# Two-layer recurrence: TensorE multiplies the middle part of layer 1's state ahead of the projection of x instead of behind it

## What is computed

```
a = x[t] @ Wx + b + h @ Wh                       # layer 0, 4 gates
c = sigmoid(a_f) * c + sigmoid(a_i) * tanh(a_g)
h = sigmoid(a_o) * tanh(c)
x1[t] = x[t] + h
m = concat([x1[t], s]) @ W1 + bias               # layer 1, 2 parts
g = sigmoid(m_g + 1);  s = g * s + (1 - g) * tanh(m_c)
out[t] = x1[t] + s
```

## Time and profile before

| | |
|---|---|
| three executions | 228.25, 232.16, 232.23 us; median 232.16 |
| profiled execution | 228.34 us, of which span 226.2 us |
| granted TensorE clock | 0.998 of full speed |
| TensorE busy | 221.1 us (98%), 4850 products |
| weight loads busy | 206.6 us (91%) |
| VectorE busy | 198.8 us (88%), 1555 instructions |
| ScalarE busy | 134.1 us (59%), 903 instructions |
| DMA | 26 GB/s from HBM over the span |

### The profile page before, as it was taken

The page is one execution under the profiler, slowest core; times in us unless marked ns, Lnnn a source line. Parts: engine busy times, 40 slices in busy tenths (PEclk is TensorE's granted clock), DMA queues, the critical chain, the costliest instruction groups (busy, mean ns, idle before and its releaser), DMA issues.

```text
span 226.2 us, 12499 instructions
## 1 busy us (share of the span) xinstructions
PE 221.1 (98%) x4850; PEld 206.6 (91%) x4850; DVE 198.8 (88%) x1555; ACT 134.1 (59%) x903; POOL 3.7 (2%) x12
## 2 busy tenths in 40 slices
PE   7999999999999999999999999999999999999994
PEld 5899999999999999999999999999999999999883
DVE  4889989899899898998998998989989989899895
ACT  3655666656566666665566566665666666656652
POOL 2400000000000000000000000000000000000000
PEclk9999999999999999999999999999999999999999
DMA  6000001010010001000010001101001000000000
GB/s 186 26 17 26 16 26 49 14 29 26 20 45 26 24 20 49 26 16 26 28 39 26 26 14 29 49 14 28 26 21 46 26 26 16 26 16 16 14 14 14
DMA packets 12006, 6.70 MB, mean 30 GB/s; under 512 B 1447, under 2 KB 11693, under 8 KB 11949
## 3 DMA queue, kind: packets, MB, share of 16 engines
q1 hardware_dynamic: 11376, 5.33, 8.4%
q10 hardware_dynamic: 572, 0.59, 0.7%
HBM read 3.82 MB, written 2.10 MB: 26 GB/s over the span
## 4 chain that ended last, share of the span: by engine, by line
DVE 79%; ACT 11%; issue 4%; PE 3%; DMA 1%; ACTq 0%
DVE cell_bank L574 13%; ACT act_bank L492 11%; DVE hT L581 8%; DVE pair L595 7%; DVE x1T L623 7%; DVE acts L603 7%; DVE scan_add L568 7%; DVE h_high L582 6%; DVE u_rest L609 6%; DVE outT L631 6%; DVE pair L597 6%; DVE h_low L588 6%; DMA xT<-in_x_dram 1%; PE a L291 1%; PE a L283 0%
## 5 line engine op out<-in xcount | busy, mean ns | idle before, releaser
L265 PE MATMUL gate_f<-hT,wh_raw 128*128 128x32 f32 x254 | 47.0, 267 | 0.3 <-DVE hT L581 0.2
L265 PEld LDWEIGHTS gate_f<-hT,wh_raw 128*128 128x128 f32 x254 | 37.8, 188 | 9.8 <-DVE hT L581 8.1
L473 ACT ACTIVATE gate_f<-gate_f 128x32 f32<-128x32 f32 x127 | 23.1, 182 | 34.2 <-PE gate_f L265 34.2
L492 ACT ACTIVATE act_bank<-cell_bank 128x32 f32<-128x32 f32 x128 | 23.3, 182 | 33.3 <-DVE cell_bank L574 33.2
L581 DVE TENSOR_TENSOR hT<-out_gate,act_bank 128x32 f32<-128x32 f32 x128 | 23.9, 187 | 21.0 <-ACT act_bank L492 21.0
L498 ACT ACTIVATE acts<-a 128x64 f32<-128x64 f32 x128 | 28.6, 223 | 17.8 <-PE a L291 4.6
L574 DVE TENSOR_TENSOR_SCAN cell_bank<-act_bank,scan_add 128x64 f32<-128x64 f32 x128 | 38.0, 297 | 0.1
L283 PE MATMUL a<-h_high,w1x_scaled 128*128 128x32 f16 x256 | 35.4, 177 | 0.2
L283 PE MATMUL a<-h_high,w1x_third 128*128 128x32 f16 x256 | 35.4, 177 | 0.0
L283 PE MATMUL a<-h_high,w1x_rest 128*128 128x32 f16 x256 | 35.4, 176 | 0.0
L285 PE MATMUL a<-h_low,w1x_fp 128*128 128x32 f16 x256 | 35.4, 176 | 0.0
(11 more groups left out here) (114 smaller groups left out, 1071.9 us busy)
## 6 DMA issues: line engine op xcount, KB each, us to landing
xT<-in_x_dram SPq DMA_DIRECT2D x45, 64.0 KB, 2.0
out_dram<-outT SPq DMA_DIRECT2D x32, 64.0 KB, 1.6
wx_s<-in_L_cond_Wx_dram SPq DMA_DIRECT2D x1, 256.0 KB, 2.9
wh_raw<-in_L_cond_Wh_dram ACTq DMA_DIRECT2D x1, 256.0 KB, 3.3
w_raw<-in_L_cond_weight_dram ACTq DMA_DIRECT2D x1, 256.0 KB, 3.5
xT<-in_x_dram ACTq DMA_DIRECT2D x1, 64.0 KB, 3.3
bias_rows<-in_biases_dram ACTq DMA_DIRECT2D x1, 3.0 KB
condT<-in_cond_dram SPq DMA_DIRECT2D x1, 16.0 KB, 3.2
```

The lines of the kernel that those rows point to most:

```text
L265: nc.tensor.matmul(gate_step(GATE_F, j), wh_raw[:, GATE_F * P:(GATE_F + 1) * P], hT[:, (j - 1) % RING, :], start=False, stop=True, skip_gr ...
L473: return nc.scalar.activation(out, gate_step(q, j), func)
L492: nc.scalar.activation(tanh_c[:, :], cell[:, :, 1], ACT.Tanh).then_inc(tanh_c_ready, 1)
```

## The change

In steps from 2 on, TensorE issues the four products with `u_rest` right behind the six products of the state's upper part, and so ahead of the projection of x at line 233. The two products with `u_low` stay behind the projection. The wait for `u_rest_ready` moves along with the products. No instruction is added or removed, and the other engines' streams are the same.

```diff
                             layer1_input(l)
                             layer1_high(r, l)
+                            layer1_rest(r, l)
 
                     ends = last and m == 1
...
                     if not (first and j < 2):
-                        layer1_rest(r, l)
                         layer1_low(r, l)
```

## The result

| | before | changed |
|---|---|---|
| median | 230.25 us (6 executions, 228.18 to 232.39) | 234.99 us (6 executions, 232.97 to 237.10) |
| profiled execution | 228.34 us, span 226.2 | 232.97 us, span 230.8 |
| eight steps, `hT` to `hT` | 13.43 us | 13.74 us |

The changed kernel is slower: the ratio is 1.0207, with a 95% interval of 1.0187 to 1.0227; whether it is slower by more than 2% is left open by that. The executions of either kernel fall into two groups about 4 us apart (228.2 to 228.3 and 232.2 to 232.4; 233.0 to 233.1 and 236.9 to 237.1), and all ratios of this document compare the lower groups only.

A forecast was written before the change was run, and what follows sets the result against it. Layer 0's 1.67 us chain was taken to bound seven steps of eight; the change makes layer 1's loop of 1.715 us the pace. Sum: 228.34 + 4.35 + 0.3 = 233.0 us, range 230.3 to 237.0.

The forecast's parts named there:

- What bounds the kernel: Before the change: layer 0's 1.67 us chain sets the pace in seven steps of eight, layer 1's in the eighth (1.71).
- the pair's threshold: Layer 1's pair on VectorE, ahead of `keep`: starting later than about 0.47 us after `hT`, it lengthens the step by the excess.
- The loop's sum: Layer 1's loop, pair to pair through u_rest, projection, u_low and tanh: 0.74 + 0.475 + 0.24 + 0.26 = 1.715 us, every step's pace.
- the late step without a projection: Step of the kernel before (u_rest 217.41 to 217.59) giving 0.05 us to the weight load and 0.125 to the next product.
- The 15 eights: Steps 2 to 124, counted as 120 at the new pace: each eight takes 13.72 us, not 13.43, adding 4.35 us in all.
- The gap at k = 3: 0.06 us before the projection's load at k = 1 and 3, possibly an extra wait's cost: at most 2.2 us, taken as 0.3.
- The no-change rival: Layer 0 still covers layer 1's loop, for instance if TensorE loads projection weights while awaiting u_rest: 227.7 to 229.1 us; chance 0.16.
- The slower-still rival: TensorE's queue tail at odd k also makes the forget product late: up to 3.6 us more, 236.6 us; chance 0.15.
- The chances: Forecast 0.66, no change 0.16, slower still 0.15, faster 0.03; turned into slower 0.48, same 0.49, faster 0.03.
- the last: The faster rival: u_rest always in time, k = 7 step from 1.71 to 1.67, 0.6 us; chance 0.03.
- The range's upper end: Whole kernel's time: 237.0 us, widened from the cost bounds' 236.7 for an execution in the upper group.

The follow-up runs named there:

- the run without those projections: Changed kernel without layer 1's projections of x at the end of odd steps (one in sixteen stays): 1.0216 of the kernel before, profiled 233.43 us.
- the version built on these: Kernel before with the new order at k = 6; at k = 7 layer 1's projection ahead of u_rest products, output gate's at the step's end: 0.9996.

## Why the prediction was right

**What bounds the kernel** held: `keep` at the later of the forget gate and the pair, and the pair's threshold near 0.47. The changed kernel's pair at 0.52 gives steps of 1.72.

**The loop's sum** was 1.715 and measured 1.717 (13.74 / 8), over pieces taken from other places: the late step without a projection gave 0.05 from `u_rest` to its load, which is 0.05 here (112.41 to 112.46), and 0.125 from there to the projection's product, which is 0.12 here (112.46 to 112.58). The wait for `u_rest` stands ahead of every projection, the pair is at 0.51 to 0.52 in every step, and no eighth step stands out, all as forecast. The 15 eights by 0.29 gave 4.35, and 0.31 was measured, 4.65 in all; 119 steps run at the new pace where 120 were counted.

**The gap at k = 3** was priced at 0.3 and is worth nothing. In the changed kernel the projection follows the last `u_rest` product without any at k = 3, wait for x and all:

```profile
109.12 0.18 PE L291 MATMUL a<-u_rest,w1h_rest 128*128 128x32 bf16 x1
109.12 0.30 PEld L233 LDWEIGHTS gate_i<-xT,wx_s 128*128 128x128 f32 x2
```

In all steps with k = 1 and 3 that load follows by 0.00 to 0.01, and these steps are no longer than the others (1.72). So 0.3 too much here and 0.3 too little in the eights cancelled: that the sum came within 0.1 us of the measured time is luck; that the loop's 0.29 per eight was near the measured 0.31 is not. The Trainium skill (Perfetto Trace Analysis, Identifying Dependency Chains) says that separate semaphore instructions may be inserted for additional waits. Whether one stands here no row shows, but behind a wait for `u_rest` it costs nothing that could be seen.

**The no-change rival** fell: the projection's load (112.56) comes behind the blocked `u_rest` products in every step, never less than 0.14 us after the end of `u_rest`. The Trainium skill (TensorE: Matmul & The Clock Gate, Step-by-step: what each phase is for) has weight loads pulled ahead of running products. In this trace the projection's load never passes the load that waits for `u_rest`.

**The slower-still rival** named a real effect, a forget gate at 0.71 to 0.72 behind odd steps, that costs nothing, as the run without those projections shows.

**The chances** put half of the forecast above 2% and half below; 1.0207 with an interval down to 1.0187 lies on that edge. Their sum has a slip: half of the forecast and the no-change rival alone give the 0.49 for same, and "most of the last" is counted only under faster. The range's upper end, 237.0, was widened for executions that are 1.7% longer, for which the prediction had no reason.

## What to carry to other kernels

When an in-order queue holds filler work, the filler belongs ahead of the wait for the value that is not ready yet. Moved behind that wait, the same filler enters the dependent loop. It first uses up that loop's slack (here 0.30 us entered and 0.04 us a step were paid), and from there on every bit of it is paid in full, even if no engine's share of busy time changes. Moved to the end of the queue, it can make the other loop late instead. To price such a move, close the loop of each recurrence by itself, from rows of the places where the order already stands that way, and compare the loops: the slower one is the pace, and a loop within 0.04 us of it (2.4% here) has next to no room. And a queue's tail that runs late costs nothing as long as another chain is later still; take it away before calling it a cause.

## What the hardware showed that was not expected

The start of an execution comes out in one of two ways, with 4 us between them. A profiled execution with the long start (the new order at k = 6 only, 232.13 us) has its fifth `hT` at 18.74 us, that of the kernel before (228.34 us) has it at 14.99; from there on their mean steps agree (1.678 and 1.679). Weight loads of TensorE in order of time, the long start first:

```profile
7.57 0.55 PEld L260 LDWEIGHTS gate_o<-condT,wh_raw 128*128 128x128 f32 x2 [0.22 <-issue]
8.85 0.50 PEld L265 LDWEIGHTS gate_f<-hT,wh_raw 128*128 128x128 f32 x2 [0.28 <-DVE hT L584]
12.32 0.55 PEld L265 LDWEIGHTS gate_f<-hT,wh_raw 128*128 128x128 f32 x2
...
15.14 0.50 PEld L265 LDWEIGHTS gate_f<-hT,wh_raw 128*128 128x128 f32 x2
...
17.28 0.30 PEld L265 LDWEIGHTS gate_f<-hT,wh_raw 128*128 128x128 f32 x2
```

```profile
6.38 0.30 PEld L260 LDWEIGHTS gate_o<-condT,wh_raw 128*128 128x128 f32 x2
7.39 0.30 PEld L265 LDWEIGHTS gate_f<-hT,wh_raw 128*128 128x128 f32 x2 [0.47 <-DVE hT L581]
9.82 0.30 PEld L265 LDWEIGHTS gate_f<-hT,wh_raw 128*128 128x128 f32 x2
```

In the first a pair of float32 weight loads takes 0.50 to 0.55 us up to 15 us and 0.30 from 17 us on; in the profiles with the short start it takes 0.30 from 6 us at the latest. The three profiles with the long start, of three kernels, all show it; the long loads end at 15 us, at 16 (the version built on these) and at 18 (the kernel before with narrower projections). The products lengthen in part only: from a float32 projection of 128 columns to the next product's start lie 0.57 us (11.96 to 12.53) and not 0.31 (9.62 to 9.93), while fp16 products of 32 columns start 0.02 to 0.03 apart in both.

What makes the start long is open. The granted clock reads 1.00 of full speed in these stretches of both profiles, so by the rows the clock is not shown as the cause. With five added products at the start none of 23 executions had the long one, where 8 of 23 beside them did; that those products act through TensorE's gaps is argued, not shown.
